# A feed-forward pass of a transformer kernel: moments written ahead of the next group's reads, reads and normalisation in halves, down rows read together, last attention period reordered

## What is computed

```python
x = x + attention(layernorm(x), Wq, Wk, Wv, Wo)
x = x + ffn(layernorm(x), gate_cp, up_cp, down_cp)
x = x + linear_attention(layernorm(x), Wq, Wk, Wog, Wig, g_weight)
x = x + ffn(layernorm(x), gate_cp, up_cp, down_cp)

def ffn(h, gate_cp, up_cp, down_cp):       # inner size 1024
    gate_w, up_w, down_w = (spline_reconstruct(cp) for cp in (gate_cp, up_cp, down_cp))
    return (silu(h @ gate_w.T) * (h @ up_w.T)) @ down_w.T
```

## Time and profile before

| | |
|---|---|
| median of 3 runs | 816.4 us (816.14 to 816.53) |
| the profiled execution | 817.79 us, span 816.1 us, mean granted PE clock 0.974 |
| busy in the span | PE 94%, DVE 75%, ACT 59%, POOL 30% |
| attention | to 367 us |
| first feed-forward pass | 367 to 517 us |
| linear attention | to 661 us |
| second feed-forward pass | 661 to 816 us |

### The profile page before, as it was taken

How to read it: one execution, slowest core, us unless ns; L and a number is a source line. 1 busy time by engine, 2 the same in 40 slices (tenths; PEclk the granted TensorE clock), 3 DMA queues, 4 the chain that set the end, 5 groups by cost and what they waited for, 6 DMA issues and landing times.

```text
span 816.1 us, 19285 instructions
## 1 busy us (share of the span) xinstructions
PE 766.9 (94%) x6818; PEld 659.2 (81%) x6818; DVE 614.4 (75%) x1269; ACT 481.5 (59%) x935; POOL 245.3 (30%) x337
## 2 busy tenths in 40 slices
PE   7789999999999999969999989999999989999998
PEld 7667777777777777647989879899999969888887
DVE  5578887777787788836888777689999667777755
ACT  3055555555555555655666657577878846666543
POOL 4047752232222333221000010157776550000000
PEclk9799999999999999977999999999999989999999
DMA  6866657666686655567666651000035144777731
GB/s 163 115 125 95 102 98 115 90 96 92 83 149 97 100 88 90 149 235 243 216 219 239 248 195 70 1 1 2 2 108 187 40 182 179 271 269 261 263 136 52
DMA packets 70983, 111.47 MB, mean 137 GB/s; under 512 B 7062, under 2 KB 27959, under 8 KB 70855
## 3 DMA queue, kind: packets, MB, share of 16 engines
q1 hardware_dynamic: 68848, 108.47, 50.8%
q10 hardware_dynamic: 2048, 1.88, 1.2%
HBM read 41.82 MB, written 42.81 MB: 104 GB/s over the span
## 4 chain that ended last, share of the span: by engine, by line
PE 58%; DMA 11%; DVE 10%; SPq 8%; ACT 6%; issue 6%; ACTq 0%; DVEq 0%; POOL 0%; POOLq 0%
PE bank L417 9%; PE bank L419 7%; PE bank L418 7%; DMA stk<-fx 5%; PE pair_a L938 5%; SPq L607 4%; DVE inter L1972 4%; PE bank L952 3%; PE pair_b L907 3%; DMA fx<-fs 3%; PE bank L1278 3%; PE pair_b L1278 3%; SPq L490 2%; PE pair_a L1243 2%; DMA stack<-mrow 2%
## 5 line engine op out<-in xcount | busy, mean ns | idle before, releaser
L417 PE MATMUL bank<-wd_hi,in_hi 128*128 128x256 f32 x512 | 146.6, 286 | 1.1 <-DVE in_lo L1977 0.9
L419 PE MATMUL bank<-wd_hi,in_lo 128*128 128x256 f32 x512 | 145.7, 285 | 0.0
L418 PE MATMUL bank<-wd_lo,in_hi 128*128 128x256 f32 x512 | 145.4, 284 | 0.0
L1794 DVE TENSOR_REDUCE mx<-pair_b 128x6 f32<-128x768 f32 x124 | 117.9, 951 | 33.9 <-PE pair_b L919 31.9
L683 POOL TENSOR_SCALAR_AFFINE_SELECT prob<-prob 128x512 f32<-128x512 f32 x128 | 81.8, 639 | 202.5 <-ACT prob L1405 202.3
L1570 ACT ACTIVATE in_hi<-inter 128x512 fp32r<-128x512 f32 x128 | 80.7, 630 | 104.8 <-DVE inter L1972 103.5
L1405 ACT ACTIVATE prob<-pair_a 128x768 f32<-128x768 f32 x128 | 103.6, 810 | 64.1 <-PE pair_a L938 62.5
L1977 DVE TENSOR_TENSOR in_lo<-inter,in_hi 128x512 fp32r<-128x512 f32 x128 | 88.4, 690 | 60.8 <-ACT in_hi L1570 59.3
L417 PEld LDWEIGHTS bank<-wd_hi,in_hi 128*128 128x128 f32 x512 | 97.8, 191 | 6.6 <-DVE in_lo L1977 1.7
L418 PEld LDWEIGHTS bank<-wd_lo,in_hi 128*128 128x128 f32 x512 | 97.6, 191 | 4.7
L419 PEld LDWEIGHTS bank<-wd_hi,in_lo 128*128 128x128 f32 x512 | 97.6, 191 | 0.0
(11 more groups left out here) (232 smaller groups left out, 1937.5 us busy)
## 6 DMA issues: line engine op xcount, KB each, us to landing
stk<-fx SPq DMA_DIRECT2D x128, 252.0 KB
stack<-stage SPq DMA_DIRECT2D x184, 128.0 KB, 4.5
fx<-fs SPq DMA_DIRECT2D x32, 512.0 KB, 3.6
fx<-fs SPq DMA_DIRECT2D x32, 256.0 KB, 3.7
fx<-fs SPq DMA_DIRECT2D x16, 504.0 KB
fx<-fs SPq DMA_DIRECT2D x16, 252.0 KB
X<-in_attn_a_x SPq DMA_DIRECT2D x14, 256.0 KB, 5.4
result<-X SPq DMA_DIRECT2D x7, 512.0 KB, 7.9
```

Source lines behind the costliest of these rows:

```text
L417: pe.matmul(dst, l_hi, r_hi, start=first, stop=False)
L418: pe.matmul(dst, l_hi, r_lo, start=False, stop=False)
L419: return pe.matmul(dst, l_lo, r_hi, start=False, stop=last)
L1794: dve.tensor_reduce(mx[:, h, :, p % PR, :], src[:, :, 0:3 * P].rearrange("p n (t k) -> p n t k", t=3), AX.X, ALU.max).then_inc(a_mx, 1)
```

## The change

On SP in the feed-forward passes the order of a period becomes: x of g + 2, moments of g + 2, second half (four transfers) of the read of g + 1, store, first half of the read of g + 2. Each half has its own semaphore for each u, and waits for the up products that used the same half of the buffer two groups before; PE waits for a half at m = 0 and at m = 4. The reads of groups 0 and 1 are issued before the loop. `normalise4` runs two tiles at m = 4 and two at m = 5.

At the hand-over, all 16 down transfers are issued together in the period of sequence 14, and x of group 0 right behind them, ahead of the max rows of 15. In the last period the first half of the read of group 0, x of group 1, the second half, moments of group 1 and x of group 2 follow the max rows of the second half. Transposes of group 2's input are taken over one step earlier (p = 6 instead of 7) by ACT and DVE; its normalisation moves from ACT to DVE at p = 2; the split of the down rows moves to p = 0, 2, 4, 6; a Silu of one column is made on ACT behind the last exponential; PE gets `keep_clock(8)` in five steps of the last period and in the first two steps of group 0, with waits for the banks that they write.

```diff
--- before.py
+++ after.py
@@ -192,6 +192,7 @@
         cst = sb("cst", [NFX, 2, MT, P], F32R)
         wd_hi = sb("wd_hi", [P, MT, D], F32R)
         wd_lo = sb("wd_lo", [P, MT, D], F32R)
+        silu_first = sb("silu_first", [P, 1], F32)
         mom = sb("mom", [P, CT, MT * KG], F32)
         mom_hi = sb("mom_hi", [P, CT, MT * KG], F32R)
         mom_lo = sb("mom_lo", [P, CT, MT * KG], F32R)
@@ -363,8 +364,9 @@
             f.gp, f.upp, f.dp = own("gp", MT), own("upp", MT), own("dp", MT + 1)
             f.pe = [f.xT, f.mp, f.gp, f.upp, f.dp]
 
-            f.xw, f.mw, f.ld = own("xw", 64), own("mw", 32), own("ld", 16 * MT)
-            f.sp = [f.xw, f.mw, f.ld]
+            f.xw, f.mw = own("xw", 64), own("mw", 32)
+            f.ld = [[own(f"ld{u}{half}", 4 * MT) for half in range(2)] for u in range(2)]
+            f.sp = [f.xw, f.mw] + f.ld[0] + f.ld[1]
             return f
 
         f_ = ffn_semaphores()
@@ -565,19 +567,26 @@
                 if nxt2:
                     stack_half(b + 2, u, 0)
                 if nxt and not nxt2:
-                    load_down(range(KG // 2))
+                    load_down(range(KG))
+                    f1_write_x(0, 0)
                 if nxt:
                     max_rows(b + 1, 1 - u, 0)
                 if nxt2:
                     stack_half(b + 2, u, 1)
+                if not nxt:
+                    sp.wait_ge(s_zeros, 32)
+                    sp.wait_ge(a_stp, upto(a_stp, B - 2, NP))
+                    f1_read(0, 0, 0)
+                    f1_write_x(1, 1)
+                    f1_read(0, 0, 1)
+                    f1_write_moments(1, 1)
+                    f1_write_x(2, 0)
                 if b in (1, 2):
                     sp.wait_ge(s_zero, 1)
                     sp.dma_start(copies[b - 1, :, D, :].rearrange("v (p k) -> v p k", k=32),
                                  zeros[48 * (b - 1):48 * b, :]).then_inc(s_zeros, 16)
                 if nxt and not nxt2:
-                    f1_write_x(0, 0)
                     f1_write_moments(0, 0)
-                    load_down(range(KG // 2, KG))
 
             copies = fx[:, 0:3 * FROWS, :].rearrange("u (v q) t -> u v q t", q=FROWS)
 
@@ -589,7 +598,9 @@
 
                 def write_x(g, u):
                     sp.wait_ge(f_.xl, upto(f_.xl, base + g, CT))
-                    sp.wait_ge(f_.ld, upto(f_.ld, base + g - 2, 16 * MT))
+                    for half in range(2):
+                        sp.sem_inc(passed_sp, 1)
+                        sp.wait_ge(f_.ld[u][half], upto(f_.ld[u][half], base + g - 2 - u, 8 * MT))
                     for c in range(CT):
                         write(u, c, P * c, P, f_.xw)
 
@@ -597,26 +608,29 @@
                     sp.wait_ge(f_.ml, upto(f_.ml, base + g, 1))
                     write(u, CT, 2 + 2 * FSTEP, P - 2, f_.mw)
 
-                def read(g, u):
+                def read(g, u, half):
                     sp.wait_ge(f_.xw, upto(f_.xw, base + g, 64))
                     sp.wait_ge(f_.mw, upto(f_.mw, base + g, 32))
-                    sp.wait_ge(f_.upp, upto(f_.upp, base + g - 1, 1))
-                    for m in range(MT):
+                    sp.sem_inc(passed_sp, 1)
+                    sp.wait_ge(f_.upp, upto(f_.upp, base + g - 2, MT // 2 * (half + 1)))
+                    for m in range(MT // 2 * half, MT // 2 * (half + 1)):
                         at = 2 + KG * m
                         rows = fx[u, at:at + 9 * FSTEP, :].rearrange("(r q) t -> r q t", q=FSTEP)[:, 0:NB, :]
-                        sp.dma_start(stk[0:NFX, u, m, :].bitcast(F32), rows).then_inc(f_.ld, 16)
+                        sp.dma_start(stk[0:NFX, u, m, :].bitcast(F32), rows).then_inc(f_.ld[u][half], 16)
 
                 def period(g, u, prev=True, nxt=True, nxt2=True, nxt3=True):
                     if nxt2 and prev:
                         write_x(g + 2, u)
-                    if nxt:
-                        read(g + 1, 1 - u)
+                    if nxt2:
+                        write_moments(g + 2, u)
+                    if nxt and prev:
+                        read(g + 1, 1 - u, 1)
                     if prev:
                         store(g - 1)
                     else:
                         first()
                     if nxt2:
-                        write_moments(g + 2, u)
+                        read(g + 2, u, 0)
 
                 return write_x, write_moments, read, run_pairs(period)
 
@@ -634,19 +648,18 @@
             f1_write_x, f1_write_moments, f1_read, run_f1 = ffn(0, lambda g: None, load_gla_constants)
             f2_write_x, f2_write_moments, f2_read, run_f2 = ffn(PAIRS, store, lambda: None)
             run_periods(sp, period)
-            f1_write_x(1, 1)
-            sp.wait_ge(s_zeros, 32)
-            sp.wait_ge(a_stp, upto(a_stp, B - 2, NP))
-            f1_read(0, 0)
-            f1_write_moments(1, 1)
-            f1_write_x(2, 0)
             sp.wait_ge(a_stp, upto(a_stp, B - 1, NP))
+            for half in range(2):
+                f1_read(1, 1, half)
             run_f1(sp)
             f2_write_x(0, 0)
             f2_write_moments(0, 0)
-            f2_read(0, 0)
+            for half in range(2):
+                f2_read(0, 0, half)
             f2_write_x(1, 1)
             f2_write_moments(1, 1)
+            for half in range(2):
+                f2_read(1, 1, half)
             f2_write_x(2, 0)
             run_f2(sp)
             for h in range(2):
@@ -743,7 +756,7 @@
                         f1_rstd(0)
                     if p == 5 and nxt and not nxt2:
                         f1_rstd(1)
-                    if p == 2 and not nxt:
+                    if p == 1 and not nxt:
                         f1_rstd(2)
 
 
@@ -1139,6 +1152,11 @@
                     if not nxt:
                         if p == 0:
                             pe.wait_ge(a_mx, upto(a_mx, B - 1, NP))
+                            pe.wait_ge(a_res, upto(a_res, B - 3, 1))
+                        if p == 2:
+                            pe.wait_ge(a_ml, upto(a_ml, b, 2))
+                        if p < 6 and p != 1:
+                            keep_clock(8, bank_p)
                         if p in (1, 5):
                             if p == 5:
                                 pe.wait_ge(f_.ml, upto(f_.ml, 1, 1))
@@ -1182,8 +1200,9 @@
 
                 def period(g, u, prev=True, nxt=True, nxt2=True, nxt3=True):
                     for m in range(MT):
-                        if m == 0:
-                            pe.wait_ge(f_.ld, upto(f_.ld, base + g, 16 * MT))
+                        if m % (MT // 2) == 0:
+                            landed = f_.ld[u][m // (MT // 2)]
+                            pe.wait_ge(landed, upto(landed, base + g - u, 8 * MT))
                         pe.wait_ge(f_.si, upto(f_.si, base + g, m - 1))
                         pe.matmul(pair_a[:, m % 2, :], cst[:, 0, m, :], stk[0:NFX, u, m, :], start=True,
                                   stop=True).then_inc(f_.gp, 1)
@@ -1333,8 +1352,11 @@
                 if m == 0:
                     pe.wait_ge(a_at, upto(a_at, B - 1, 1))
                     turn_o(B - 1, 1)
+                    keep_clock(8, bank_t)
                 if m == 1:
                     turn_att(B - 1)
+                    pe.wait_ge(a_res, upto(a_res, B - 2, 1))
+                    keep_clock(8, bank_p)
                 if m == 2:
                     pe.wait_ge(a_res, upto(a_res, B - 2, 1))
                     proj_out(B - 1)
@@ -1506,18 +1528,18 @@
                             f1_high_x(0, p - 2, (bank_t, bank_p)[p - 2])
                         if p == 5:
                             f1_high_moments(0, bank_p)
-                        if p == 6:
-                            f1_normalise(1)
+                        if p in (6, 7):
+                            f1_normalise(1, range(TB * (p - 6), TB * (p - 5)))
                     if not nxt:
-                        if p in (1, 7):
+                        if p == 7:
+                            act.activation(silu_first[:, :], quarter[:, :], ACT.Silu)
+                        if p in (1, 6):
                             for c in range(CT):
                                 f1_high_x(1 + p // 4, c, pair_b[:, c, :])
                         if p == 3:
                             f1_high_moments(1, pair_b[:, 0, :])
-                        if p == 4:
-                            f1_normalise(2)
-                        if p in (2, 4, 6, 7):
-                            high_down((p - 1) // 2)
+                        if p in (0, 2, 4, 6):
+                            high_down(p // 2)
                     if p == 0:
                         if prev:
                             copy_o(b - 1, 1)
@@ -1538,11 +1560,11 @@
             attention = period
 
             def ffn(base, ahead, tail, first):
-                def normalise4(g):
+                def normalise4(g, tiles=range(2 * TB)):
                     act.wait_ge(f_.mr, upto(f_.mr, base + g, 1))
```

(21 more changed lines are left out.)

## The result

The changed kernel took 806.6 us (median of 9 runs, 804.3 to 810.9) beside 814.3 for the kernel before on the same chips: ratio 0.990, 95% interval 0.9876 to 0.9933. Its profiled execution took 804.9 us, span 803.1. The forecast was 801.4, in a range of 792.5 to 808.0. So the change is faster, the time lies inside the range, and the gain by the medians is 7.7 us, half of the expected 15. The two profiles differ by 13.0 us of span, and the starts of the gate matmuls give the sum: the max rows of the period before the last went out at 323.16 instead of 325.63 (2.5 us that were there in the first 50 us already, no part of the change); from there to group 1 it took 65.7 us instead of 63.0, so **the hand-over lost 2.7**; from group 1 to the start of group 7 the first pass gained 5.1, and the second pass from group 1 on gained 7.8 (0.2 us lie between them).

What follows compares the result with a forecast made beforehand. PE's waits for late stacked-row reads, with PE and the DMA engines behind them, were taken to bound it. Gains of 11.5 (feed-forward) and 3.5 (hand-over) took 817.8 to 802.8, less 1.4 is 801.4 us; range 792.5 to 808.

Steps and rivals of the forecast that it cites:

- Feed-forward, 11.5 us: Both feed-forward passes: earlier reads remove each group's stall, gaining 5.4 us in the first and 6.1 in the second; bounds 5 and 14.
- the floor: Feed-forward groups 1 to 4: a group that waits for nothing takes 17.79 us, taken as PE's own limit.
- Normalisation in halves: Feed-forward, m = 4 and 5: same four activations, less in front of a Silu; 0 to 0.3 us a group.
- Rival B: Feed-forward: nine DMA engines keep groups 1 to 4 at 18.5 us, only groups 5 and 6 gain; 805.3 us, chance 0.20.
- C: Feed-forward rival: second half of the reads lands too late behind the moments write; slower, 821.8 us, chance 0.07.
- D: Rival for the whole kernel: hand-over at its lower bound together with B, little change, 812 to 818 us; chance 0.05.
- Hand-over, a gain of 3.5: From the last attention period to feed-forward group 1: net gain 3.5 us, bounds -2 and +10.
- Delay of the max rows: Last attention period: max rows queue on SP behind sixteen down loads and the x write, costing 9.3 us.
- A: Hand-over rival: max rows are not held; hand-over gains 7.5 to 8 us, total 797 us, chance 0.22.
- Waits that go: Hand-over: ACT's 5.07 and 1.99 us waits and 2.08 us of normalisation leave the ACT-PE chain, 9.1 us.
- Clock: Last attention period: keeping the clock up, 0.76 from 353.0 on, should return about 1.2 us.
- Wait of ACT for the second x write: Last attention period: ACT's early second half waits about 1 us for the write of x(1); bounds 0 and 3.

Runs made afterwards that it cites:

- after_again: The changed kernel measured once more, nothing altered: 808.9 us, ratio 0.990 to the kernel before.
- rows_on_act: Changed kernel, but ACT issues the max rows of the last attention period on its own queue: 804.6 us, ratio 0.986 to the kernel before.
- early_x1: Changed kernel, but down loads issued four to a period in four earlier periods, x of group 1 written before group 0's first read: 794.2 us, 0.974.
- x1_first: Changed kernel, but SP issues the x write of group 1 ahead of the first half of group 0's read: 802.7 us, ratio 0.984.
- late_x2: Changed kernel, but ACT and DVE split the third x block at p = 7 again instead of p = 6: 803.3 us, ratio 0.985.
- early_x1_nokeep: Changed kernel with down loads in four earlier periods and the second x write first, without the added dummy matmuls: 794.4 us, ratio 0.976.

## Why the prediction was right and where it failed

The time lies in the range with some luck. The hand-over's -2.7 us are outside its own bounds (-2 and +10), the feed-forward part gave 1.5 more than taken, for another reason than mine, and the profile after had 2.5 us of its gain from elsewhere.

**Feed-forward, 11.5 us: right in size (13.0 in the profile, 13.6 alone), wrong in its reason.** The failed step is the floor. I took 17.79 us, a group that waits for nothing, for PE's own time, and the waits of the earlier trace rows for the whole stall. But the next group, 443.88 to 463.05, took 19.17 with a wait of 0.24: 1.4 us that no wait explained, which stood in the rows I had chosen. They were the loop of ACT and DVE, 18.77 us a group, catching up on PE; a group that neither of the two delays takes 17.5 (388.89 to 406.39 in the kernel after). So groups 1 to 4 gained 4.0 and 3.6 us (taken 2.6 and 1.3, and at most 3.2 and 2.8). Groups 5 gained 2.75 and 2.1 (2.5 and 1.9), group 6 of the second pass 2.8 (2.9): right. Group 6 of the first pass, priced at a gain of 0.3, took 1.6 longer, and from group 7 of the second pass to the end it was 0.7 longer.

**Normalisation in halves, 0 to 0.3 us a group: the worst-sized term.** It is worth 0.5 alone and 1.0 beside the new order of the reads. I priced its length on ACT and didn't ask who waits behind it.

**Rival B, nine engines bound the groups: fell.** The groups run at 17.6 us with a DMA share of 0.72 in the second pass. **C** fell: the second half is never late. **D** fell with B.

**Hand-over, a gain of 3.5: a loss of 2.7 in the profile, about 6 in the runs.** By its terms, in the profile, corrected by the 2.5 us of the earlier start:
- Delay of the max rows: 9.3 taken, 6.5 measured (343.93 + 2.47 against 339.91) and more in the slow drain of after_again, PE's wait being 3.3 longer there. Right in place and about in size, and A fell. The reason was right in part: ring order accounts for some 2.6 us, and the loads hold the rows on another queue too (rows_on_act).
- Waits that go, 9.1: without the two stalls (early_x1) the period still takes 18.6 us from first scores to group 0, which follows the last weighing at once, where 24.8 (339.91 to 364.7) less 9.1 would be 15.7. They were worth 6.2; what fills the rest no run separates.
- Clock: 1.2 expected back inside the period. Those 18.6 us are at full clock already, so nothing comes on top of the 6.2. And while PE stood for the max rows it fell, to 0.62 in the mean from 341 to 350 (1.00 in early_x1 from 340 to 350), and the first two steps took 5.8 us instead of 3.4: 2.4 lost.
- Wait of ACT for the second x write: 1.0 taken, 3 at the most, and 4.7 and 5.7 measured. I had named the step, and bounded it without following SP to the issue of the write, which stands behind four reads and is late by all that the max rows are late. x1_first and late_x2 show it from both sides.
- Group 0: 20.4 us from the last weighing to group 1 taken, 19.4 measured.

Sum: 2.9 + 2.4 + 3.7 - 2.8 + 1.2 - 1.0 = 6.4, and 3.5 - (-2.7) is 6.2.

## What to carry to other kernels

Before a wait's time is booked as gain, look at whether the stretches without a wait are as short as the work in them: two loops of about one length (here reads at 18.1 us, ACT and DVE at 18.6) hide one another, and taking away one alone gives nothing or half. An activation put into such a loop cost nothing here while it filled the gap of ACT (1.08 us), and 0.9 us when it was longer (2.06), so cut it to the gap. Keep bulk loads away from the moment at which small rows decide, and when a wait is moved ahead of other work, follow the transfer it waits for to its place in the queue.

## What the runs showed of the hardware

- Four tiny loads on a queue of their own didn't pass sixteen loads of another queue (issued by 339.15, moved after 343.5), but got past the x write issued behind those loads (PE waited 7.01 us, and 9.5 to 9.7 where they stood behind it at the same rate of drain).
- The same sixteen loads drained at 91 and at 71 GB/s in two executions of one kernel, at a DMA share of 0.56 and 0.58, and at 76 and 81 in other runs; PE's wait for rows behind them went from 6.4 to 9.7 us with it.
- A write of moments behind one store of 512 KB landed after 9.7 us; in the first pass of the kernel after, which stores nothing, the x writes of 256 KB took 5.5 in the median.
- The granted clock was 0.62 in the nine microseconds from 341 on, after PE had stood 6.4 us. With no such stand (early_x1_nokeep) it stayed at 1.00, and the dummy matmuls made no difference there.
- The early Silu began 0.02 us behind a table load of 1.28 us (367.11, 368.41). The Trainium skill's page "ScalarE: Activation LUTs", section "What ACT_TABLE_LOAD costs", gives 1283 ns and 1380 ns of drain; the trace agrees with the first and shows no drain at this switch.
